# Decoder layer on one core: the 35 rounds of self-attention written out, and one transposition of the slot stage moved into the next projection

## The chip, the cores and the metric

The kernel runs on one core of one Trainium2 chip, as one program for a whole post-norm decoder layer. The metric is the device time of one execution in microseconds, from the kernel's runs on the chip; lower is better. The core's engines are TensorE (PE in the rows; PEld is its loading of weights), VectorE (DVE), ScalarE (ACT), GpSimd (POOL) and SyncE (SP, which here issues most DMAs). Each engine has its own stream of instructions, and they wait for each other by semaphores only.

## The reference, cut to what matters

```python
# x (8, 512, 512), ctx_1024 (8, 512, 512); H = 16 heads
# self-attention with relative positions, D = 32
scores = jnp.einsum('bhqd,bhkd->bhqk', q, k)
rel_q = jnp.einsum('bhld,lrd->bhlr', q, pos_emb)
rel_k = jnp.einsum('bhrd,lrd->bhlr', k, pos_emb)
probs = jax.nn.softmax((scores + rel_q + rel_k) / sqrt(D), axis=-1)
out = layernorm(ctx(probs, v) @ Wo + bo + x)
x = _layernorm(x + out)
...
x = _layernorm(x + cross_attention(x, ctx_1024))     # 16 heads of 64, causal
# slot layer: 16 slots per batch attend to the tokens, one expert per slot, tokens attend to the slots
o = q + _mha(q, x, x, d_Wq, ..., d_Wo, d_bo)          # q: slot_query, 16 rows per batch
...
x = _layernorm(x + _mha(x, o, o, c_Wq, ..., c_Wo, c_bo))
```

## The kernel before

The program is a row of stages with a barrier between them: `self_attention` (its first 1,900 us), `project_norm` (its output projection and two norms), `cross_attention`, `norm_and_slots` (cross-attention's projection and norm, together with the slots' attention over the tokens), `experts`, and `slots_to_tokens`. The change touches the first and the fourth.

**Self-attention.** The work is cut into 32 quads (`QUADS`): a quad is four heads of one batch. A round `g` of an engine is one call of its `quad(g, j)`, 16 steps `i` (four heads, four tiles of 128 query rows), and `j` is `g % 4`, which picks buffers. The stages of the pipeline lie up to two quads apart, so the rounds go from -2 to 32, 35 in all. In a step TensorE does `score` (L225, L227), `bands` for a later step (L251 to L257, the relative-position products that go out to DRAM and come back sheared by DMA), a share of the projections (L275, L286, L321, L324), and `turn` (L237), the transposition of an earlier tile of probabilities; VectorE's copy at L478 (`v_out`) stands once in each round, at its step 2. The order of these pieces is fixed by tables (`Q_AT`, `KV_AT`, `STACK_TICKS` and others), which the change leaves alone. `steps` is what calls `quad`, on each of the five engines: rounds -2, -1 and 0 are written out, rounds 1 to 24 are a hardware loop (`Fori`) of three passes whose body is eight rounds, and rounds 25 to 32 are written out again. Inside the loop `g` is a register, so the numbers that waits compare with and the addresses of some DMAs are worked out by register instructions; outside it they are constants.

**The slot stage.** `norm_and_slots` goes over 32 tiles of 128 tokens, one for each step `s`; four tiles are a batch `b`. On TensorE a step is `project(s)` (L1249, eight logical matmuls of 128x512 that the trace shows as 16), and `turn(s - 2)` (L1259, the transposition of a normed tile). Every fourth step adds `scores(b)` (L1292), the one after it `turn_probs(b, 0)` and `turn_probs(b, 1)` (both L1301: the batch's two tiles of slot probabilities are transposed, one after the other, into the same PSUM tile `ps_t`), and the next `mix(b)` (L1312). Between the two, ScalarE's `pt_out` (L1509) has to copy the first tile out of `ps_t`, and it does so behind the norm of a token tile (L1494) in its own queue.

Of the kernel before, what the change touches and what calls it, by code (L numbers as in the profile page):

```python
# [13 lines left out]
K4 = E // P  # L14
# [3 lines left out]
QUADS = B * (H // HQ)  # L18
# [31 lines left out]
def self_attention(nc, dr, sem, keep):  # L50
# [6 lines left out]
    with ExitStack() as ctx:  # L57
# [44 lines left out]

        def steps(e, quad):

            for g in (-2, -1, 0):
                quad(g, g % 4)
            with e.Fori(1, QUADS - 7, 8) as g:
                for j in range(8):
                    quad(g + j, (1 + j) % 4)
            for g in range(QUADS - 7, QUADS + 1):  # L110
                quad(g, g % 4)

        def ahead(g, j, i):
# [7 lines left out]
        def _(sp):  # L121
# [83 lines left out]
            for c in range(2):  # L205
                sp.dma_start(okv[c][:, :, :, :].rearrange("p a k n -> p (a k n)"), dr["b_wkv"](c))\
                    .then_inc(sem[f"a_okv_in{c}"], 16)
            steps(sp, quad)
            sp.wait_ge(sem["a_stored"], 16 * QUADS + 16)
            for i in range(2):  # L210
# [3 lines left out]
        def _(pe):  # L214
# [141 lines left out]

            pe.wait_ge(sem["a_wq_in"], 16 * K4)
            steps(pe, quad)

        @block.scalar  # L360
        def _(act):
# [64 lines left out]
            act.wait_ge(sem["a_cols_in"], 16)  # L426
            act.wait_ge(sem["a_bk_in"], 16)
            steps(act, quad)

        @block.vector  # L430
# [167 lines left out]
UNITS = B * T4  # L598
# [536 lines left out]
def norm_and_slots(nc, dr, sem, first, keep):  # L1135
# [5 lines left out]
    with ExitStack() as ctx:  # L1141
# [6 lines left out]
        R, CT, CH = 6, 4, 2 * K4  # L1148
        SCORES, TURNS, MIX = T4 + 3, T4 + 4, T4 + 5
# [33 lines left out]
        def at(s, lag):  # L1183

            return (s - lag) // T4 if (s - lag) % T4 == 0 and 0 <= s - lag < UNITS else None
# [55 lines left out]

        @block.tensor
        def _(pe):
            def project(u):
                pe.wait_ge(sem[f"f_in{u % R}"], 32 * (u // R) + 32)
                if u >= 2:
                    pe.wait_ge(sem["f_summed"], u - 1)
                for k in range(CH):
                    mm = pe.matmul(ps_o[u % 2][:, :], cT[u % CT][:, k, :], w[:, k, :], start=(k == 0), stop=(k == CH - 1))  # L1249
                mm.then_inc(sem["f_projected"], 1)  # L1250

            def turn(u):
                pe.wait_ge(sem["f_y"], u + 1)
                if u == 0:
                    pe.wait_ge(sem["f_const_in"], 16)
                if u:
                    pe.wait_ge(sem["f_yT"], u)
                for k in range(K4):
                    mm = pe.transpose(ps_y[:, k * P:(k + 1) * P], y[u // T4 % 2][:, u % T4, k * P:(k + 1) * P], ident[:, :])  # L1259
                mm.then_inc(sem["f_turned"], 1)  # L1260

            def queries():
                pe.wait_ge(sem["f_setup_in"], 64)
                for m in range(K4):
                    for k in range(K4):
                        mm = pe.matmul(ps_m[:, 0, m * NS:(m + 1) * NS], wq[:, k, m * P:(m + 1) * P], sqT[:, k, :],
                                       start=(k == 0), stop=(k == K4 - 1))
                mm.then_inc(sem["f_q_ready"], 1)

            def folded():  # L1270
                pe.wait_ge(sem["f_qd"], 1 + K4 * HQ)
                for m in range(K4):
                    mm = pe.matmul(ps_m[64 * (m % 2):64 * (m % 2) + 64, 1, m // 2:m // 2 + 1],
                                   qd[:, m, :, :].rearrange("p h s -> p (h s)"), cols[:, 1, m:m + 1],
                                   start=True, stop=True)
                mm.then_inc(sem["f_cb_ready"], 1)
                for k in range(K4):
                    for m in range(K4):
                        mm = pe.matmul(ps_s[:, k // 2, (k % 2) * HS + m * 64:(k % 2) * HS + (m + 1) * 64],
                                       wkT[:, m, k * P:(k + 1) * P], qd[:, m, :, :].rearrange("p h s -> p (h s)"),  # L1280
                                       start=True, stop=True)
                mm.then_inc(sem["f_a_ready"], 1)

            def scores(b):
                pe.wait_ge(sem["f_yT"], T4 * b + T4)
                if b == 0:
                    pe.wait_ge(sem["f_a"], 1)
                else:
                    pe.wait_ge(sem["f_scaled"], 2 * b)
                for i in range(2):  # L1290
                    for k in range(K4):
                        mm = pe.matmul(ps_s[:, i, :], a[:, k, i * P:(i + 1) * P], yT[b % 2][:, k, :],  # L1292
                                       start=(k == 0), stop=(k == K4 - 1))
                    mm.then_inc(sem["f_scored"], 1)

            def turn_probs(b, i):
                pe.wait_ge(sem["f_probs"], 2 * b + i + 1)
                if b or i:
                    pe.wait_ge(sem["f_pt"], 2 * b + i)
                for r in range(T4):  # L1300
                    mm = pe.transpose(ps_t[:, r * P:(r + 1) * P], sc[b % 2][:, i, r * P:(r + 1) * P], ident[:, :])  # L1301
                mm.then_inc(sem["f_probs_turned"], 1)

            def mix(b):
                pe.wait_ge(sem["f_pt"], 2 * b + 2)
                if b:
                    pe.wait_ge(sem["f_mixed_out"], b)
                else:
                    pe.wait_ge(sem["f_a"], 1)
                for k in range(K4):  # L1310
                    for r in range(T4):
                        mm = pe.matmul(ps_m[:, k // 2, (k % 2) * HS:(k % 2 + 1) * HS], y[b % 2][:, r, k * P:(k + 1) * P],  # L1312
                                       pt[:, r, :], start=(r == 0), stop=(r == T4 - 1))
                mm.then_inc(sem["f_mixed"], 1)

            pe.wait_ge(sem["f_w_in"], 16)
            for s in range(STEPS):
                if s < UNITS:
                    project(s)
                if s == SETUP:  # L1320
                    queries()
                if s == SETUP + 1:
                    folded()
                if at(s, TURNS) is not None:
                    turn_probs(at(s, TURNS), 0)
                if 0 <= s - 2 < UNITS:
                    turn(s - 2)
                if at(s, TURNS) is not None:
                    turn_probs(at(s, TURNS), 1)
                if at(s, SCORES) is not None:  # L1330
                    scores(at(s, SCORES))
                if at(s, MIX) is not None:
                    mix(at(s, MIX))
            pe.wait_ge(sem["f_mixed_out"], B)
            pe.wait_ge(sem["f_end_in"], 96)
            for m in range(K4):
                for k in range(K4):
                    for hh in range(HQ):
                        c = HQ * m + hh
                        mm = pe.matmul(ps_s[D * hh:D * (hh + 1), 0, m * SB:(m + 1) * SB], wv[:, k, c * D:(c + 1) * D],  # L1340
                                       mixed[:, :, k, c * NS:(c + 1) * NS].rearrange("p b s -> p s b"),
                                       start=(k == 0), stop=(k == K4 - 1))
            mm.then_inc(sem["f_cx_ready"], 1)
            pe.wait_ge(sem["f_cx"], 1)
            for m in range(K4):
                mm = pe.matmul(ps_s[:, 1, :], cx[:, m, :], wo[:, m, :], start=(m == 0), stop=(m == K4 - 1))
            mm.then_inc(sem["f_o_ready"], 1)
            pe.wait_ge(sem["f_h"], 3)
            for k in range(K4):
                mm = pe.transpose(ps_t[:, k * P:(k + 1) * P], h[:, k * P:(k + 1) * P], ident[:, :])  # L1350
# [851 lines left out]
```

## Time and profile before

| | |
|---|---|
| median of 3 runs | 3918.7 us (3915.43 to 3924.49) |
| profiled execution, its own time | 3919.53 us |
| its span, first to last instruction | 3917.9 us |
| mean granted clock of TensorE | 0.954 |
| instructions in the trace | 65,917 |
| busy: TensorE, VectorE, GpSimd, ScalarE | 3508.0, 2177.9, 1823.9, 1770.2 us |

The busy time of an engine is the sum over its instructions, and its share of the span says how near it is to being the bound on average. The granted clock is 1.00 where TensorE runs at its upper level of 2.4 GHz and 0.50 where it runs at 1.2 GHz. "Idle before" is the time that an engine stood still ahead of an instruction; the name behind the arrow is what ended it, and "issue" there means that nothing in the profile was being waited for.

### The profile page before, as it was taken

Reading aid. Unit: us, or ns where it says so; the run is one execution under the profiler, and the core shown is the slowest. Engines: PE = TensorE matmul, PEld = TensorE weight load, DVE = VectorE, ACT = ScalarE, POOL = GpSimd, SP = SyncE. Lnnn points to the kernel's source line nnn. Section 1 sums busy time; section 2 is a strip of 40 time slices with the busy share of each in tenths; the row PEclk is TensorE's granted clock in tenths of the full one; section 3 lists DMA queues with packets and bytes.
Section 4 is the critical chain, followed back from the end, with each engine's and each line's share of the span. In section 5 each row is a group of like instructions: output and inputs, shape, how many; then the busy total and the mean of one; then the engine's idle time right before and its main releaser. Section 6 shows DMA issues by size and latency. Waiting matters only on the chain. (4 is left out here: it accounts for less than half of the span.)

```text
span 3917.9 us, 65917 instructions
## 1 busy us (share of the span) xinstructions
PE 3508.0 (90%) x19744; PEld 2239.2 (57%) x19744; DVE 2177.9 (56%) x5890; ACT 1770.2 (45%) x3799; POOL 1823.9 (47%) x1652
## 2 busy tenths in 40 slices
PE   6999989999899999999897999999899986565588
PEld 4777767777677777777444555555455541111154
DVE  4666656666566666666686666666433321211267
ACT  4666656666566666666355555555212210000024
POOL 3666656666566666666325777777411100000012
PEclk8999999999999999999998999999999998888799
DMA  7999998999899999999793223222345319999914
GB/s 280 386 386 382 380 386 339 387 380 381 341 386 383 380 383 385 379 389 385 253 275 115 84 85 95 84 84 73 120 149 199 113 42 415 417 417 418 376 65 172
DMA packets 429722, 1091.96 MB, mean 279 GB/s; under 512 B 25152, under 2 KB 107584, under 8 KB 380224
## 3 DMA queue, kind: packets, MB, share of 16 engines
q1 hardware_dynamic: 412208, 1040.34, 71.0%
q10 hardware_dynamic: 16656, 47.19, 3.1%
q8 instruction: 162, 2.65, 0.3%
q14 instruction: 184, 1.51, 0.1%
q0 software_dynamic: 512, 0.26, 0.0%
HBM read 650.97 MB, written 436.73 MB: 278 GB/s over the span
## 5 line engine op out<-in xcount | busy, mean ns | idle before, releaser
L553 POOL TENSOR_SCALAR a_sc<-a_sc,a_inv 128x512 f32<-128x512 f32 x512 | 823.9, 1609 | 585.3 <-DVE a_inv L496 540.8
L505 DVE COPY a_pt<-a_ps_t 128x512 f32<-128x512 f32 x512 | 353.5, 690 | 547.8 <-PE a_ps_t L237 530.4
L1096 POOL TENSOR_SCALAR b_sc<-b_sc,b_inv 128x128 f32<-128x128 f32 (+3 forms) x512 | 547.3, 1086 | 181.1 <-DVE b_inv L1065 177.8
L375 ACT ACTIVATE a_stage_q<-a_ps_b 128x640 f32<-128x640 f32 x512 | 360.8, 705 | 587.6 <-PE a_ps_b L255 552.9
L1026 ACT ACTIVATE b_sc<-b_sc,b_mx 128x128 f32<-128x128 f32 (+3 forms) x512 | 282.0, 552 | 317.0 <-DVE b_mx L1059 316.7
L365 ACT ACTIVATE a_sc<-a_sc,a_mx 128x512 f32<-128x512 f32 x512 | 370.0, 723 | 54.8 <-DVE a_mx L489 51.4
L489 DVE CUSTOM_DVE_ANT_0 a_sc<-a_ps_s,a_rq 128x512 f32<-128x512 f32 x512 | 353.1, 690 | 74.6 <-PE a_ps_s L227 59.3
L375 ACT ACTIVATE a_stage_k<-a_ps_b 128x640 f32<-128x640 f32 x512 | 357.4, 698 | 0.0
L237 PEld LDWEIGHTS a_ps_t<-a_ident,a_sc 128*128 128x128 f32 x2048 | 247.6, 141 | 146.5 <-issue 141.1
L1059 DVE CUSTOM_DVE_ANT_0 b_sc<-b_ps_s,b_mask 128x128 f32<-128x128 f32 (+3 forms) x512 | 229.5, 488 | 166.0 <-PE b_ps_s L974 162.2
L237 PE MATMUL a_ps_t<-a_ident,a_sc 128*128 128x128 f32 x2048 | 308.9, 274 | 8.8 <-DVE a_pt L505 8.8
L227 PE MATMUL a_ps_s<-a_ident,a_rk 128*128 128x128 f32 x2048 | 307.6, 273 | 0.0
L324 PEld LDWEIGHTS a_ps_o<-a_okv,keep 128*128 128x128 f32 x2048 | 263.2, 191 | 76.8 <-issue 72.2
L227 PEld LDWEIGHTS a_ps_s<-a_ident,a_rk 128*128 128x128 f32 x2048 | 256.3, 141 | 37.8 <-issue 1.2
L1710 POOL DMA_DIRECT2D y<-d_y x16 | 8.6, 535 | 577.1 <-DVE d_y L1681 577.1
L275 PE MATMUL a_ps_c<-a_xT,keep 128*128 128x512 f32 x512 | 256.4, 605 | 21.9 <-DVE a_lo_q L459 12.1
L324 PE MATMUL a_ps_o<-a_okv,keep 128*128 128x128 f32 x2048 | 269.5, 276 | 1.8 <-ACT a_kv L397 1.8
L321 PE MATMUL a_ps_o<-keep,a_okv 128*128 128x512 f32 x512 | 266.6, 607 | 0.4 <-ACT a_kv L400 0.4
L960 PE MATMUL b_ps_q<-b_xT,keep 128*128 128x512 f32 x512 | 260.5, 612 | 6.8 <-PEq L2124 6.8
L225 PE MATMUL a_ps_s<-a_ks,a_qs 128*128 128x512 f32 x512 | 248.1, 485 | 17.1 <-issue 11.7
L1072 DVE COPY b_pt<-b_ps_t 128x128 f32<-128x128 f32 (+3 forms) x512 | 226.9, 485 | 63.7 <-PE b_ps_t L982 63.7
L1249 PE MATMUL f_ps_o<-keep,f_cT 128*128 128x512 f32 x512 | 234.8, 614 | 9.3 <-DMA f_x<-x 9.3
(215 smaller groups left out, 6227.0 us busy)
## 6 DMA issues: line engine op xcount, KB each, us to landing
band_q<-a_stage_q SPq DMA_DIRECT2D x128, 1280.0 KB, 6.8
band_k<-a_stage_k SPq DMA_DIRECT2D x128, 1280.0 KB, 9.9
a_rk<-band_k SPq DMA_DIRECT2D x128, 1024.0 KB, 12.7
a_rq<-band_q SPq DMA_DIRECT2D x256, 512.0 KB, 13.4
d_w<-in_e_W SPq DMA_DIRECT2D x24, 4096.0 KB, 42.9
d_wg<-in_e_Wg SPq DMA_DIRECT2D x16, 4096.0 KB, 28.5
keep<-in_e_W SPq DMA_DIRECT2D x8, 4096.0 KB, 36.3
a_okv<-in_b_wkv ACTq DMA_DIRECT2D x62, 512.0 KB, 7.9
```

The lines of the kernel that those rows point to most:

```text
L227: mm = pe.matmul(out[:, r * P:(r + 1) * P], rk[h][:, r, t * P:(t + 1) * P], ident[:, :], is_transpose=True, start=False, stop=(r == T4 - 1))
L237: mm = pe.transpose(ps_t[:, r * P:(r + 1) * P], sc[i % SC][:, r * P:(r + 1) * P], ident[:, :])
L321: mm = pe.matmul(ps_o[:, :], okv[c][:, 0, n, :], oc[:, n, :], start=(n == 0), stop=(n == K4 - 1))
L324: mm = pe.matmul(ps_o[:, n * P:(n + 1) * P], oc[:, k, n * P:(n + 1) * P], okv[c][:, 1, k, :], start=(k == 0), stop=(k == K4 - 1))
L365: act.activation(sc[n][:, :], sc[n][:, :], ACT.Exp, bias=mx[:, n:n + 1], scale=-1.0, accum_out=sm[:, n:n + 1]).then_inc(sem["a_exped"], 1)
L375: act.activation(st[h % 2][:, t, :], src, ACT.Copy).then_inc(sem[f"a_{kind}_staged"], 1)
L489: dve.tensor_tensor_reduce(out=sc[n][:, :], in0=ps_s[i % 2][:, :], in1=rq[rn][:, i % 2, :], scale=-SCALE_A, scalar=BIG, op0=ALU.add, op1=A ...
L505: dve.tensor_copy(pt[:, h % 2, :, t * P:(t + 1) * P], ps_t[:, :].rearrange("p (r n) -> p r n", r=T4)).then_inc(sem["a_pt_out"], 1)
L553: pool.tensor_scalar(sc[n][:, :], sc[n][:, :], inv[:, n:n + 1], None, ALU.mult)\
L960: mm = pe.matmul(ps_q[:, :], wq[:, j % XP, k, :], xT[j // XP][:, k, :], start=(k == 0), stop=(k == K4 - 1))
L1026: act.activation(sc[j % 2][i][:, 0:width(i)], sc[j % 2][i][:, 0:width(i)], ACT.Exp, bias=mx[j % 2][:, i:i + 1], scale=-1.0, accum_out=sm[j ...
L1096: pool.tensor_scalar(sc[j % 2][i][:, 0:width(i)], sc[j % 2][i][:, 0:width(i)], inv[j % 2][:, i:i + 1], None, ALU.mult).then_inc(sem["b_nor ...
```

## The change

Two edits. `steps` calls `quad` for all 35 rounds with numbers instead of a loop, on all five engines, so there is no jump and no register in self-attention. And in the slot stage `project` is cut into two halves of four matmuls, and `turn_probs(b, 1)` goes from the end of its step to between the halves of the next step's projection.

```diff
         def steps(e, quad):
 
-            for g in (-2, -1, 0):
-                quad(g, g % 4)
-            with e.Fori(1, QUADS - 7, 8) as g:
-                for j in range(8):
-                    quad(g + j, (1 + j) % 4)
-            for g in range(QUADS - 7, QUADS + 1):
+            for g in range(-2, QUADS + 1):
                 quad(g, g % 4)
...
-            def project(u):
-                pe.wait_ge(sem[f"f_in{u % R}"], 32 * (u // R) + 32)
-                if u >= 2:
-                    pe.wait_ge(sem["f_summed"], u - 1)
-                for k in range(CH):
+            def project(u, half):
+                if half == 0:
+                    pe.wait_ge(sem[f"f_in{u % R}"], 32 * (u // R) + 32)
+                    if u >= 2:
+                        pe.wait_ge(sem["f_summed"], u - 1)
+                for k in range(K4 * half, K4 * half + K4):
                     mm = pe.matmul(ps_o[u % 2][:, :], cT[u % CT][:, k, :], w[:, k, :], start=(k == 0), stop=(k == CH - 1))
-                mm.then_inc(sem["f_projected"], 1)
+                if half:
+                    mm.then_inc(sem["f_projected"], 1)
...
                 if s < UNITS:
-                    project(s)
+                    project(s, 0)
+                if at(s, MIX) is not None:
+                    turn_probs(at(s, MIX), 1)
+                if s < UNITS:
+                    project(s, 1)
...
                     turn_probs(at(s, TURNS), 0)
                 if 0 <= s - 2 < UNITS:
                     turn(s - 2)
-                if at(s, TURNS) is not None:
-                    turn_probs(at(s, TURNS), 1)
                 if at(s, SCORES) is not None:
                     scores(at(s, SCORES))
```

TensorE at the end of the loop's body in the kernel before: the last products of a round, then the loop's own two instructions, and then the written-out round 25.

```order
L324 MATMUL a_ps_o<-a_okv,keep 128x128 x4
L237 MATMUL a_ps_t<-a_ident,a_sc 128x128 x4
L107 REGISTER_ALU
L107 COMPARE_AND_BRANCH
L225 MATMUL a_ps_s<-a_ks,a_qs 128x512
L227 MATMUL a_ps_s<-a_ident,a_rk 128x128 x4
L251 MATMUL a_ps_b<-a_eq,a_qs 128x384
```

TensorE in the changed kernel where round 8 ends and round 9 begins, the place where the loop jumped back (lines of the changed kernel stand five lower in self-attention).

```order
L319 MATMUL a_ps_o<-a_okv,keep 128x128 x4
L232 MATMUL a_ps_t<-a_ident,a_sc 128x128 x4
L220 MATMUL a_ps_s<-a_ks,a_qs 128x512
L222 MATMUL a_ps_s<-a_ident,a_rk 128x128 x4
L246 MATMUL a_ps_b<-a_eq,a_qs 128x384
L249 MATMUL a_ps_b<-a_eq,a_qs 128x256
```

The matmuls and their order are the same in both; the register instruction and the branch between two rounds are gone, and so are those within the rounds.

TensorE in the slot stage before, from one batch's probabilities (L1301) to its mixing (L1312); f_ps_t is `ps_t`, f_ps_o the projection's tile, f_ps_y that of a normed token tile.

```order
L1249 MATMUL f_ps_o<-keep,f_cT 128x512 x8
L1301 MATMUL f_ps_t<-d_ident,f_sc 128x128 x4
L1259 MATMUL f_ps_y<-d_ident,f_y 128x128 x4
L1301 MATMUL f_ps_t<-d_ident,f_sc 128x128 x4
L1249 MATMUL f_ps_o<-keep,f_cT 128x512 x8
L1259 MATMUL f_ps_y<-d_ident,f_y 128x128 x4
L1312 MATMUL f_ps_m<-f_pt,f_y 128x256 x16
```

The same stretch in the changed kernel.

```order
L1245 MATMUL f_ps_o<-keep,f_cT 128x512 x8
L1298 MATMUL f_ps_t<-d_ident,f_sc 128x128 x4
L1256 MATMUL f_ps_y<-d_ident,f_y 128x128 x4
L1245 MATMUL f_ps_o<-keep,f_cT 128x512 x4
L1298 MATMUL f_ps_t<-d_ident,f_sc 128x128 x4
L1245 MATMUL f_ps_o<-keep,f_cT 128x512 x4
L1256 MATMUL f_ps_y<-d_ident,f_y 128x128 x4
L1309 MATMUL f_ps_m<-f_pt,f_y 128x256 x16
```

The second tile's transposition has moved behind four matmuls of the projection that used to follow it. For the last two batches there is no projection left in the next step, and the order is what it was.

## Rows read from the trace of the kernel before

**Rows 1.** The page: busy time, two DMA queues, the slot stage's projection.
```profile
PE 3508.0 (90%) x19744; PEld 2239.2 (57%) x19744; DVE 2177.9 (56%) x5890; ACT 1770.2 (45%) x3799; POOL 1823.9 (47%) x1652
...
q8 instruction: 162, 2.65, 0.3%
q14 instruction: 184, 1.51, 0.1%
...
L1249 PE MATMUL f_ps_o<-keep,f_cT 128*128 128x512 f32 x512 | 234.8, 614 | 9.3 <-DMA f_x<-x 9.3
```

**Rows 2.** Windows: engines' busy time, then granted clock, DMA share, GB/s.
```profile
580.00:590.00 10.00, 5.74 (x19) 4.56 (x20) 2.72 (x6) 2.60 (x5) 2.77 (x3) 0.50 0.67 239
1521.15:1747.28 226.13, 223.71 (x1473) 172.91 (x1472) 147.49 (x349) 142.82 (x281) 142.81 (x129) 1.00 1.01 386
```

**Rows 3.** Timeline of TensorE behind the loop's first jump: start, duration, idle before.
```profile
581.20 0.79 PE L225 MATMUL a_ps_s<-a_ks,a_qs 128*128 128x512 f32 x1 [5.83 <-issue]
...
586.22 0.37 PE L254 MATMUL a_ps_b<-a_eq,a_qs 128*128 128x256 f32 x1 [3.06 <-issue]
```

**Rows 4.** Timeline of VectorE: the copy that stands once in each round.
```profile
527.92 0.69 DVE L478 COPY a_v<-a_ps_c 128x512 f32<-128x512 f32 x1 [0.45 <-PE a_ps_c L286]
598.06 0.69 DVE L478 COPY a_v<-a_ps_c 128x512 f32<-128x512 f32 x1 [0.45 <-PE a_ps_c L286]
...
767.74 0.69 DVE L478 COPY a_v<-a_ps_c 128x512 f32<-128x512 f32 x1 [0.46 <-PE a_ps_c L286]
825.17 0.69 DVE L478 COPY a_v<-a_ps_c 128x512 f32<-128x512 f32 x1 [0.45 <-PE a_ps_c L286]
...
995.22 0.69 DVE L478 COPY a_v<-a_ps_c 128x512 f32<-128x512 f32 x1 [0.45 <-PE a_ps_c L286]
1065.67 0.69 DVE L478 COPY a_v<-a_ps_c 128x512 f32<-128x512 f32 x1 [0.46 <-PE a_ps_c L286]
...
1521.15 0.69 DVE L478 COPY a_v<-a_ps_c 128x512 f32<-128x512 f32 x1 [0.52 <-PE a_ps_c L286]
...
1747.28 0.69 DVE L478 COPY a_v<-a_ps_c 128x512 f32<-128x512 f32 x1 [0.52 <-PE a_ps_c L286]
```

**Rows 5.** Timeline of the slot stage: one batch from norm to mixing.
```profile
2963.15 0.60 PE L1259 MATMUL f_ps_y<-d_ident,f_y 128*128 128x128 f32 x4
...
2970.45 0.60 PE L1259 MATMUL f_ps_y<-d_ident,f_y 128*128 128x128 f32 x4
...
2984.63 0.60 PE L1301 MATMUL f_ps_t<-d_ident,f_sc 128*128 128x128 f32 x4
...
2985.06 0.60 PE L1259 MATMUL f_ps_y<-d_ident,f_y 128*128 128x128 f32 x4
...
2987.57 0.58 ACT L1509 ACTIVATE f_pt<-f_ps_t 128x512 f32<-128x512 f32 x1
2988.29 1.08 PE L1301 MATMUL f_ps_t<-d_ident,f_sc 128*128 128x128 f32 x4 [2.63 <-ACT f_pt L1509]
...
2989.17 8.01 PE L1249 MATMUL f_ps_o<-keep,f_cT 128*128 128x512 f32 x16
...
2997.02 0.60 PE L1259 MATMUL f_ps_y<-d_ident,f_y 128*128 128x128 f32 x4
...
3011.24 0.60 PE L1259 MATMUL f_ps_y<-d_ident,f_y 128*128 128x128 f32 x4
```

**Rows 6.** The same timeline: L1259 beside the probabilities of batches 0, 3 and 5.
```profile
2890.01 0.60 PE L1259 MATMUL f_ps_y<-d_ident,f_y 128*128 128x128 f32 x4
...
3033.15 0.60 PE L1259 MATMUL f_ps_y<-d_ident,f_y 128*128 128x128 f32 x4
...
3043.71 0.60 PE L1259 MATMUL f_ps_y<-d_ident,f_y 128*128 128x128 f32 x4
...
3128.21 0.60 PE L1259 MATMUL f_ps_y<-d_ident,f_y 128*128 128x128 f32 x4
...
3140.28 0.60 PE L1259 MATMUL f_ps_y<-d_ident,f_y 128*128 128x128 f32 x4
```

## Prediction

> **What bounds the kernel now.** I read the page first. TensorE is busy for 90% of the span, and no other engine for more than 56% [rows 1], so time is to be had where TensorE stands still or runs slowly. Windows of 10 us over self-attention came next. They are full of TensorE work at a clock of 1.00 nearly everywhere, and fall to about half at two places, near 575 and near 1045 us; the first is shown, with 5.74 us of work at a clock of 0.50 [rows 2]. The timeline at that place shows TensorE idle for 5.83 us and, five microseconds later, for another 3.06 us, both times put down to "issue": nothing in the profile was being waited for [rows 3]. VectorE and ScalarE stand still at the same moment. It is the point where all five engines jump back to the head of the loop: three passes make two jumps, and there are two such places. The loop is entered and left without a gap of this kind.
>
> In the slot stage I read the projection's group and the timeline of one batch. The projection waited for a DMA only once, 9.3 us at the stage's start [rows 1], and TensorE goes without a gap through the steps, but for one place in each batch: 2.63 us ahead of the second transposition of probabilities, until ScalarE has copied the first tile out [rows 5].
>
> **The change, part by part. The jumps.** The copy at L478 is a clock for the rounds. The round with the first jump takes 598.06 - 527.92 = 70.14 us, and the round at the same place of the pattern of four, without a jump, 825.17 - 767.74 = 57.43; the jump costs 12.71 us. The second: 1065.67 - 995.22 = 70.45, less 57.43, is 13.02 us [rows 4]. That is all of it: the two idles (8.9 us in the first case) and TensorE's work at half clock between and behind them. The sum is 25.7 us. After the edit no engine has a branch there, and the instructions of both sides are the ones that run today. I take all of it, since no other work lies under it: TensorE is what stands still, and the rounds before and after are full.
>
> **The register instructions.** Written-out rounds exist in the trace of before: 25 to 32. Four of them take 1747.28 - 1521.15 = 226.13 us; the same four places in the loop take 825.17 - 598.06 = 227.11. That is 0.98 us for four rounds, and 24 rounds move over, so 6 x 0.98 = 5.9 us. Another way to read it: from 598.06 to 1065.67 are eight rounds, 467.61 us with one jump, without it 454.59, against twice 226.13 = 452.26; 2.3 us for eight rounds or 7.0 for 24 [rows 4]. From below nothing, if the difference is the place in the stage and not the registers. I take 5.9, which both readings are near, with 0 and 7.0 as bounds.
>
> What could take it back is the fetching of instructions. The two instruction queues moved 2.65 + 1.51 = 4.16 MB for 65,917 instructions, 63 bytes each [rows 1]: what runs is fetched as it runs, in the loop on each pass too. So the written-out program fetches about as much, and somewhat less for the register instructions that go. The written-out rounds 25 to 32 ran at full clock with 223.71 us of TensorE work in 226.13 [rows 2], so fetching straight code was hidden under them. The DMA side can't catch its breath any more at a jump, and its engines read 1.01 busy in those rounds [rows 2]. But rounds 17 to 32 already run 16 in a row, and their length doesn't creep up; 32 in a row should not either.
>
> The Trainium skill (Runtime: NRT & Kernel Launch, Instruction fetch mechanics) says that prefetch is sequential and that a taken branch out of the present pages waits for the fetch of its target page. By that rule one jump is one wait; the row shows two, 5.83 and 3.06 us [rows 3]. If the second were an ordinary page boundary and stayed, some 3 us and a part of the slow clock would be kept at each place, and the gain would be 25.7 less 3.1 and 3.1, or 19.5, and the sum 48.6. The same instructions ran in the first pass, entered without a jump, and had no such idle, so I side with the trace and count both.
>
> **The moved transposition.** From one L1259 to the next over a plain step takes 2970.45 - 2963.15 = 7.30 us, and a transposition of four adds 2985.06 - 2984.63 = 0.43. So the stretch from L1259 of the probabilities' step to the next should take 7.73 us with `turn_probs` in it. It takes 2997.02 - 2985.06 = 11.96 us [rows 5], and 3043.71 - 3033.15 = 10.56 in the mildest batch, 3140.28 - 3128.21 = 12.07 in the last that counts [rows 6]. The difference between 10.56 and the others is the clock: behind the idle of 2.63 us the projection took 2997.02 - 2989.17 = 7.85 us until the next L1259, against 7.30 - 0.43 = 6.87 in a plain step, and the transposition itself 1.08 instead of 0.60 [rows 5]. For all six batches: 3128.21 - 2890.01 = 238.20 us over five periods is 47.64 each [rows 6]; without the stall a period is 7.73 + (3011.24 - 2997.02 = 14.22) + 7.30 + (2985.06 - 2970.45 = 14.61) = 43.86 [rows 5]. Five times 3.78 is 18.9, and the sixth batch gives 12.07 - 7.73 = 4.3. Together 23.2 us. Batches 6 and 7 keep their order and give nothing.
>
> Does the moved piece wait anew? Its first half-projection starts at 2985.06 + 0.43 and takes (7.30 - 0.43) / 2 = 3.44 us, so TensorE comes to it at 2988.93. ScalarE's copy ends at 2987.57 + 0.58 = 2988.15, and the row shows the transposition starting at 2988.29 [rows 5]. The margin is 0.64 us. The copy stands behind the norm of a token tile (L1494) on ScalarE, and nothing of the edit moves either. The second copy now waits until about 2989.4 and ends by 2990.1; behind it in ScalarE's queue stands the square root for the tile whose projection ends only near 2992.8, so nothing waits for ScalarE. `mix` needs the copy after a further transposition of tokens, at about 2993. The cover of the new copy is thus a half-projection of 3.44 us against 0.6 us of copying. If the margin fell away, what is late next is TensorE itself, by tenths of a microsecond.
>
> From below: if only the stall and not the clock came back, it is six times 10.56 - 7.73 = 2.83, 17.0 us [rows 5, 6]. From above nothing beyond 23.2, because no other gap is left there.
>
> The weights of the first expert are loaded in the middle of this stage, well ahead of its end, and the later stages keep their lengths and only start earlier.
>
> **The sum.** The profiled execution took 3919.5 us (span 3917.9 and 1.6 around it), the median of the runs is 3918.7, 0.8 lower. 25.7 + 5.9 + 23.2 = 54.8 us, so 3864.7 by the profiled execution and 3863.9 by the median. I say 3864. The bounds of this case: 19.5 + 0 + 17.0 = 36.5 us of gain at worst, 25.7 + 7.0 + 23.2 = 56 at best, 3863 to 3882 by the median, and 3 us on either side for the spread of the runs: 3860 to 3885.
>
> **Rivals.** (1) The straight rounds become bound by DMA. DMA engines read busy throughout [rows 2], and the pauses of some 12 us at the jumps are the only rest. If they were what keeps the band reads in time, the 25.7 us would be given back as waits at the scores: 3864 + 26 = 3890. Against it: 16 rounds in a row without drift. 7 in 100. (2) The slot stage keeps its wait: the moved transposition meets a late copy, or the clock falls for another reason. With the 17.0 us it is 3870, inside my range; with nothing gained there 3887. The margin of 0.64 us speaks against, but it is thin, and the early batches might differ. 7 in 100 for the loss of most of it. (3) The other side: fetching the written-out code isn't hidden. A stall of the kind seen at a jump, 12.9 us, then stands at places in the straight code. With 55 us to win, counting the two that go, it takes more than four such stalls in 24 rounds to make the kernel slower; one in every third round is eight, 103 us, and 3967. Rounds 25 to 32 had none in eight rounds, and neither had the first pass of the loop. 3 in 100. (4) The edit doesn't do what it says. The instructions in order show no branch left in self-attention, and the moved rows; 1 in 100, with 3919. My forecast has the remaining 82 in 100.
>
> **How the numbers follow.** What a measurement of this kernel can tell from no change is about 0.2%, 7.8 us: 3911 to 3926.5. The main case and the first two rivals are all below 3911. So faster 0.95, the same 0.02, slower 0.03. The range takes the main case's 3860 to 3885 and widens it below to 3856, for a gain in straight rounds that I undersized, and above to 3890, where the first two rivals end.
>
> **What would show it right or wrong.** In the profile after: no "issue" idle of several microseconds on TensorE in self-attention, and no fall of the clock near 575 or 1045 us; the copy at L478 (then L473) every 55.9 to 57.4 us in all rounds; in the slot stage no wait of the transpositions for ScalarE's copy in batches 0 to 5, and 43.9 us for a batch. Wrong would be: waits of the scores for the sheared bands, "issue" idles at regular distances in the straight rounds, or a new idle of TensorE between the halves of a projection.

## The result, and the profile after

The changed kernel takes 3861.97 us in the median of four runs (3859.88 to 3866.55), the kernel before 3921.59 in the same comparison (3915.43 to 3928.5). The ratio is 0.9856, with a 95% interval of 0.9843 to 0.9868: 1.4% faster, by 52 to 62 us. The profiled executions have spans of 3861.9 and 3917.9 us, 56.0 apart, against a forecast of 54.8.

The page of the changed kernel, where it answers to [rows 1]:

```profile
PE 3488.0 (90%) x19744; PEld 2230.2 (58%) x19744; DVE 2173.7 (56%) x5890; ACT 1768.0 (46%) x3799; POOL 1823.7 (47%) x1652
...
q8 instruction: 155, 2.54, 0.3%
q14 instruction: 150, 1.23, 0.1%
...
L1245 PE MATMUL f_ps_o<-keep,f_cT 128*128 128x512 f32 x512 | 230.9, 603 | 8.5 <-DMA f_x<-x 8.5
```

The counts of the working instructions are the same; what fell is TensorE's busy time, by 20 us, at the places where it ran at half clock before (below). The two instruction queues moved less, not more: 2.54 + 1.23 = 3.77 MB where it was 4.16.

Windows of the changed kernel, the first where the jump was, the second over four rounds that used to be in the loop:

```profile
580.00:590.00 10.00, 9.44 (x64) 6.17 (x63) 5.87 (x13) 4.80 (x9) 7.14 (x7) 1.00 1.03 390
1036.61:1263.09 226.48, 223.65 (x1473) 172.87 (x1472) 147.16 (x349) 142.93 (x281) 142.49 (x129) 1.00 1.01 385
```

Where the clock was 0.50 and TensorE did 5.74 us of work in ten [rows 2], it reads 1.00 and 9.44. The timeline of VectorE, with the copy that stands once in each round (rounds 1, 8, 9 and 25; its line is five lower than before):

```profile
130.08 0.69 DVE L473 COPY a_v<-a_ps_c 128x512 f32<-128x512 f32 x1 [0.52 <-PE a_ps_c L281]
...
525.92 0.69 DVE L473 COPY a_v<-a_ps_c 128x512 f32<-128x512 f32 x1 [0.52 <-PE a_ps_c L281]
583.19 0.69 DVE L473 COPY a_v<-a_ps_c 128x512 f32<-128x512 f32 x1 [0.52 <-PE a_ps_c L281]
...
1489.68 0.69 DVE L473 COPY a_v<-a_ps_c 128x512 f32<-128x512 f32 x1 [0.52 <-PE a_ps_c L281]
```

The round that jumped is now 57.27 us long instead of 70.14 [rows 4], and TensorE has no idle put down to "issue" in self-attention. From the first of these rows to the last are 24 rounds, 1359.60 us.

What the jump waited for can be read in the kernel before. The queue q8 carries TensorE's instructions, and q14 those of other engines: with TensorE alone written out q8 falls from 2.65 to 2.54 MB and q14 stays at 1.51, and with the other four written out it is q14 that falls, to 1.23, and q8 that stays (both kernels stand below). The DMA view of the kernel before, first for the 5.83 us of the first idle (575.37 to 581.20), then for the 3.06 of the second (583.17 to 586.22):

```profile
q8 instruction: 1, 0.02, 1.0%
```

```profile
q8 instruction: 1, 0.02, 2.7%
```

Each idle holds one packet of q8, of 16 KB (at 578.57 and 583.59 us in the trace), and ends 1.7 and 1.3 us behind that packet's end. It is the same at all eleven jumps of TensorE in the four kernels that have them (this one and three of the experiments): 22 idles, 22 packets, and 1.3 to 1.8 us from a packet's end to TensorE's next matmul. In the rounds of the changed kernel the packets of q8 come every 13 to 25 us, and TensorE does not stop for them. So both idles read as waits for instructions; no run changed the fetching alone.

The slot stage. First one batch in the timeline, to be read beside [rows 5], then windows of the changed kernel and of the kernel before, each from the first batch's first transposition of probabilities to the last L1259 (L1256) that has a projection ahead of it:

```profile
2991.11 0.60 PE L1298 MATMUL f_ps_t<-d_ident,f_sc 128*128 128x128 f32 x4
...
2991.55 0.60 PE L1256 MATMUL f_ps_y<-d_ident,f_y 128*128 128x128 f32 x4
...
2991.99 3.60 PE L1245 MATMUL f_ps_o<-keep,f_cT 128*128 128x512 f32 x8
...
2994.06 0.58 ACT L1508 ACTIVATE f_pt<-f_ps_t 128x512 f32<-128x512 f32 x1
2995.42 0.60 PE L1298 MATMUL f_ps_t<-d_ident,f_sc 128*128 128x128 f32 x4
2995.86 3.60 PE L1245 MATMUL f_ps_o<-keep,f_cT 128*128 128x512 f32 x8
2996.06 0.60 ACT L1508 ACTIVATE f_pt<-f_ps_t 128x512 f32<-128x512 f32 x1 [1.43 <-PE f_ps_t L1298]
...
2999.29 0.60 PE L1256 MATMUL f_ps_y<-d_ident,f_y 128*128 128x128 f32 x4
```

```profile
2859.50:3108.56 249.06, 249.06 (x782) 135.54 (x781) 82.56 (x184) 52.03 (x88) 25.31 (x20) 1.00 0.42 149
```

```profile
2889.57:3161.80 272.23, 256.47 (x782) 139.02 (x781) 82.58 (x184) 52.03 (x88) 25.31 (x20) 0.97 0.38 136
```

The copy ends at 2994.64 and TensorE comes for the second transposition at 2995.42, without a wait. The distance from L1256 to L1256 is 7.74 us, where it was 11.96. Over the whole stretch TensorE is busy 249.06 of 249.06 us at clock 1.00; before it was 256.47 of 272.23 at 0.97. The stretch is 23.17 us shorter with the same 782 matmul records.

Where the rest lies is read from four anchors: the first matmul of the output projection behind self-attention, and one near the end of the slot stage, in the kernel before and after:

```profile
1908.44 5.70 PE L713 MATMUL na_ps_o<-keep,na_cT 128*128 128x512 f32 x8 [9.24 <-DMA na_xT<-in_xT]
...
3226.20 0.72 PE L1350 MATMUL f_ps_t<-d_ident,f_x 128*128 128x128 f32 x4 [4.29 <-DVE f_x L1477]
```

```profile
1878.48 5.64 PE L708 MATMUL na_ps_o<-keep,na_cT 128*128 128x512 f32 x8 [9.21 <-DMA na_xT<-in_xT]
...
3171.86 0.66 PE L1349 MATMUL f_ps_t<-d_ident,f_x 128*128 128x128 f32 x4 [4.29 <-DVE f_x L1476]
```

Self-attention ends 29.96 us earlier. At the second anchor it is 54.34, so 24.4 lie between, nearly all in the slot stage; the last 1.7 us up to 56.0 came in the experts' and tokens' stages, which the change leaves alone.

### The profile page after: what moved, and what is told of

Its sections match the earlier page's. It is cut to its first block and busy times, and to the rows that moved or that the text cites. A ratio compares the mean times of both kernels' runs of the same rounds, so it can differ in the third digit from the quotient of the medians.

```text
span 3861.9 us, 63144 instructions
## 1 busy us (share of the span) xinstructions
PE 3488.0 (90%) x19744; PEld 2230.2 (58%) x19744; DVE 2173.7 (56%) x5890; ACT 1768.0 (46%) x3799; POOL 1823.7 (47%) x1652
## 3 DMA queue, kind: packets, MB, share of 16 engines
q8 instruction: 155, 2.54, 0.3%
q14 instruction: 150, 1.23, 0.1%
## 5 line engine op out<-in xcount | busy, mean ns | idle before, releaser
L270 PE MATMUL a_ps_c<-a_xT,keep 128*128 128x512 f32 x512 | 256.5, 605 | 22.6 <-DVE a_lo_q L454 12.5
## 6 DMA issues: line engine op xcount, KB each, us to landing
a_rk<-band_k SPq DMA_DIRECT2D x128, 1024.0 KB, 12.9
d_wg<-in_e_Wg SPq DMA_DIRECT2D x16, 4096.0 KB, 28.4
```

## The experiments

The theory is the forecast's: two jumps at about 12.9 us, register instructions, and six stalls with a slow clock behind them. Its rivals are that the gain comes from one of the edits alone or from the registers, that the price belongs to the loop and not to the jump, and that something other than the copy's place held the transposition. Except where it is said otherwise, a kernel has the other edit as in the kernel before.

**Each edit alone.** The first has the written-out `steps`, the second the halved projection with `turn_probs` in its middle; each is one half of the diff that is shown above.

> Only self-attention's rounds are written out; the slot stage is that of before. Theory (two jumps at 12.9 us each, register instructions some 4 to 6 us, parts add up): 30 us faster than before, ratio 0.9923. Rival (the two edits help each other, or the gain lies mostly in the slot stage): less than 20 us.

Measured: 3886.97 us (3879.98 to 3893.96) against 3917.46 beside it, 30.5 us less; ratio 0.9916 (0.9898 to 0.9934). The theory's 30 holds, and its 24 rounds take 1359.52 us (131.56 to 1491.08), as in the changed kernel.

> Only the second tile of probabilities is moved into the next projection; self-attention loops as before. Theory (six stalls of 2.63 us and the slow clock behind four of them): 23 to 24 us faster than before, ratio 0.9940, with no clock below 1.00 in the slot stage between its start and batch 6. Rival (the clock falls in that stage for another reason): 17 us or less, ratio above 0.9955.

Measured: 3895.63 us (3892.71 to 3898.25), 21.8 us less; ratio 0.9942 (0.9925 to 0.9958). The theory's 23 to 24 lie within its interval, and the rival's ratio above 0.9955 is only just inside; the stage decides: its first six batches are 43.87 us apart as in the changed kernel, and the mean granted clock from the stage's start to the seventh is 1.00. The two edits alone make 52.3 us, and both together 59.6 in one comparison and 57.2 in another (below). With intervals of some 6 us on each, the parts add up within the noise.

**Registers without a jump.** One pass over a body of 24 rounds: every wait and address still has its register.

```diff
-            with e.Fori(1, QUADS - 7, 8) as g:
-                for j in range(8):
+            with e.Fori(1, 3, 2) as g:
+                for j in range(24):
                     quad(g + j, (1 + j) % 4)
```

> Self-attention's 24 rounds as one pass of a loop whose body has all 24: g is still a register in every wait and address, but no jump is taken. Slot stage of before. Theory (jumps cost 25.7 us, registers 4 to 6): 26 us faster than before, 4 to 6 us slower than the written-out kernel of the same call. Rival (the register instructions are what cost, and the idle at the jump is made up elsewhere): no more than 10 us faster than before.

Measured: 3895.25 us (3893.9 to 3898.04), 22.2 us less than before; ratio 0.9945 (0.9929 to 0.9962), and 8.3 us behind the written-out kernel, more than was expected. The stage itself is less noisy to read than the whole. The copies of rounds 1 and 25 in this kernel, and then that of round 1 in the kernel before:

```profile
130.23 0.69 DVE L478 COPY a_v<-a_ps_c 128x512 f32<-128x512 f32 x1 [0.45 <-PE a_ps_c L286]
...
1493.12 0.69 DVE L478 COPY a_v<-a_ps_c 128x512 f32<-128x512 f32 x1 [0.52 <-PE a_ps_c L286]
```

```profile
129.85 0.69 DVE L478 COPY a_v<-a_ps_c 128x512 f32<-128x512 f32 x1 [0.45 <-PE a_ps_c L286]
```

That is 1362.89 us for the 24 rounds. Written out they are 1359.60, so the registers cost 3.3 us. In the kernel before the same rounds, from 129.85 to 1521.15 us, took 1391.30, so taking two jumps cost 28.4. The other 5 us between the two medians are not seen in the profiles: the profiled executions took 3893.9 and 3893.96 us, and there it was the written-out kernel whose `project_norm` was longer, 186.1 against 181.1 us with the same code. That stage alone varies by as much as is to be explained.

Where the 3.3 us lie can be read on TensorE. Once in each round it waits for VectorE's copy of the probabilities; in the kernel before, and in the changed one:

```profile
189.50 1.92 PE L307 MATMUL a_ps_c<-a_pt,a_v 128*32 128x512 f32 x16 [0.71 <-DVE a_pt L505]
```

```profile
189.50 1.92 PE L302 MATMUL a_ps_c<-a_pt,a_v 128*32 128x512 f32 x16 [0.56 <-DVE a_pt L500]
```

The wait is 0.70 to 0.83 us in every round with registers, this kernel's too, and 0.56 to 0.60 in written-out rounds; with TensorE alone or the other four alone written out (below) it is 0.62 to 0.68. Some 0.15 us in each of 24 rounds is 3.6, so the registers' price lies at this one place of a round.

**More jumps.** The body is four rounds, so five jumps are taken.

```diff
-            with e.Fori(1, QUADS - 7, 8) as g:
-                for j in range(8):
+            with e.Fori(1, QUADS - 7, 4) as g:
+                for j in range(4):
```

> The loop's body is four rounds instead of eight, so five jumps are taken instead of two; slot stage of before. Theory (a fixed price of 12.9 us for each jump taken): 38.6 us slower than before, ratio 1.0098. Rival A (a shorter body is still at hand for the engines and its jump is cheap): faster than before by up to 25 us. Rival B (the price belongs to the loop as such, not to the jump): no change.

Measured: 3952.14 us (3950.18 to 3957.27), 34.7 us more; ratio 1.0091 (1.0073 to 1.0108). Both rivals fall. Around the second jump, timeline of TensorE and of VectorE's copies:

```profile
594.11 0.79 PE L225 MATMUL a_ps_s<-a_ks,a_qs 128*128 128x512 f32 x1 [6.35 <-issue]
598.57 0.37 PE L254 MATMUL a_ps_b<-a_eq,a_qs 128*128 128x256 f32 x1 [2.49 <-issue]
```

```profile
540.35 0.69 DVE L478 COPY a_v<-a_ps_c 128x512 f32<-128x512 f32 x1 [0.46 <-PE a_ps_c L286]
609.87 0.69 DVE L478 COPY a_v<-a_ps_c 128x512 f32<-128x512 f32 x1 [0.45 <-PE a_ps_c L286]
```

The theory's 38.6 is 4 us too much; of the 34.7, 31.6 lie in the 24 rounds (1422.93 us). All five jumps look like this, with two idles put down to "issue", 5.8 to 6.4 us and 2.5 to 3.1. This round takes 69.52 us; the five are 69.89, 69.52, 69.45, 69.25 and 69.30, against 57.40 for the round of that place without a jump, so a jump costs 12.1 us on average.

**Whose jump it is.** `steps` gets a flag, and the engines named are written out while the others loop.

```diff
-        def steps(e, quad):
+        def steps(e, quad, written=False):
 
+            if written:
+                for g in range(-2, QUADS + 1):
+                    quad(g, g % 4)
+                return
...
-            steps(pe, quad)
+            steps(pe, quad, True)
```

> TensorE's rounds are written out, the other four engines still loop; slot stage of before. Theory (every engine stands still at its own jump for some 6 us, TensorE for a second time for 3 us, and TensorE has no slack): TensorE now waits for VectorE and ScalarE at their jumps, so about half of the two jumps' price comes back: 8 to 14 us faster than before. Rival A (TensorE's own fetch is all that counts): 26 us or more. Rival B (any engine's jump costs the full price): 0 to 3 us.

Measured: 3904.65 us (3900.56 to 3908.08) against 3920.32, 15.7 us less; ratio 0.9957 (0.9944 to 0.9971). A little above the 8 to 14 of the theory: the 24 rounds take 1374.65 us, 16.65 less than before, of which the two jumps give 12.2, rounds 6, 14 and 22, which are no longer than others here, 2.6 (below), and the shorter wait for the copy of probabilities (0.63 us) the rest. The timeline at the first jump:

```profile
581.25 0.60 ACT L404 ACTIVATE a_kv<-a_ps_o 128x512 f32<-128x512 f32 x1 [5.26 <-issue]
...
581.99 2.05 PE L325 MATMUL a_ps_o<-keep,a_okv 128*128 128x512 f32 x2 [4.38 <-ACT a_kv L404]
...
582.38 0.69 DVE L509 COPY a_pt<-a_ps_t 128x512 f32<-128x512 f32 x1 [5.79 <-issue]
```

TensorE goes on for 2.4 us, and then stands still for ScalarE, which stands still at its own jump. The copies of VectorE put this round at 64.08 us against 57.33: 6.75 us, half the price.

> TensorE still loops, the other four engines are written out; slot stage of before. Theory (TensorE's own two idles, 5.83 and 3.06 us, and the half clock between them are the price, and the others stand still under them): close to before, 0 to 5 us faster, from the register instructions of the others. Rival (the others' jumps add to TensorE's): 12 us or more faster.

Measured: 3918.06 us (3914.35 to 3920.61) against 3920.32; ratio 0.9996 (0.9986 to 1.0006). No change in the whole, as the theory had it; the 24 rounds are 3.5 us shorter (1387.82). The timeline at the first jump of this kernel:

```profile
576.54 0.69 DVE L509 COPY a_pt<-a_ps_t 128x512 f32<-128x512 f32 x1
...
581.45 0.79 PE L229 MATMUL a_ps_s<-a_ks,a_qs 128*128 128x512 f32 x1 [6.06 <-issue]
...
583.31 0.69 DVE L493 CUSTOM_DVE_ANT_0 a_sc<-a_ps_s,a_rq 128x512 f32<-128x512 f32 x1 [6.07 <-PE a_ps_s L231]
...
587.28 0.37 PE L258 MATMUL a_ps_b<-a_eq,a_qs 128*128 128x256 f32 x1 [3.88 <-issue]
```

VectorE does the copy at 576.54 at once, where the kernel before held it until 582.32 (its row has 5.82 of issue), and it gains nothing by that: it then waits 6.07 us for TensorE. Its stalls and TensorE's lay over one another. Only with all five written out did the whole price go; which engines besides TensorE are needed for that was not tried one by one.

**The margin of the moved transposition.** The changed kernel, cut after two matmuls.

```diff
-                for k in range(K4 * half, K4 * half + K4):
+                for k in ((0, 1) if half == 0 else range(2, CH)):
```

> The changed kernel with the projection cut after two of its eight matmuls instead of four. Theory (the margin ahead of the first copy is 0.64 us, and half of a half-projection is 1.72 us): TensorE comes 1.1 us too early and waits 1.1 us in each of six batches, 6 to 7 us slower than the changed kernel, or up to 14 if the clock falls behind a wait of this length. Rival (the copy is ready whenever TensorE is away from it for a moment): no change.

Measured: 3868.79 us (3867.36 to 3869.51); ratio to the kernel before 0.9866 (0.9847 to 0.9886). That is 6.8 us above the median of the changed kernel in the main comparison, as the theory had it. The second transposition of batch 1 in the timeline:

```profile
2904.22 0.63 PE L1298 MATMUL f_ps_t<-d_ident,f_sc 128*128 128x128 f32 x4 [0.91 <-ACT f_pt L1508]
```

TensorE waits 0.91 us in this batch and the ones after it, and 1.27 in batch 0; the clock stays up behind a wait of this length. The batches are 44.97 us apart where they were 43.87, so a batch loses 1.10 us against 1.1 expected; the idle in the row reads a little less than the delay, since the ends of matmuls in the profile are modelled. The margin was real, and it is thin: a cut at four has it, one at two has not.

**The wait removed from the other side.** Self-attention written out; TensorE's order of before; ScalarE copies the first tile before the square root and the norm.

```diff
             for s in range(STEPS):
+                if at(s, TURNS) is not None:
+                    pt_out(at(s, TURNS), (0,))
                 if s < UNITS:
                     std(s)
...
                 if at(s, TURNS) is not None:
-                    pt_out(at(s, TURNS))
+                    pt_out(at(s, TURNS), (1,))
```

> Self-attention written out; in the slot stage TensorE's order is that of before, and ScalarE copies the first tile of probabilities out before the square root and the norm of its step, not behind them. Theory (the 2.63 us were the copy's place in ScalarE's queue): TensorE waits some 0.5 us instead of 2.63 in batches 0 to 5 and the clock stays up, 18 to 20 us faster than the written-out kernel with the old slot stage, 4 us slower than the changed kernel. Rival (delaying the norm delays the token tiles' transpositions and so TensorE elsewhere): no faster than the written-out kernel.

Measured: 3863.4 us (3860.29 to 3866.21); ratio 0.9853 (0.9833 to 0.9874). Its timeline:

```profile
2944.64 0.60 PE L1296 MATMUL f_ps_t<-d_ident,f_sc 128*128 128x128 f32 x4
...
2945.08 0.60 PE L1254 MATMUL f_ps_y<-d_ident,f_y 128*128 128x128 f32 x4
...
2945.28 0.60 ACT L1504 ACTIVATE f_pt<-f_ps_t 128x512 f32<-128x512 f32 x1 [4.98 <-PE f_ps_t L1296]
...
2946.02 0.63 PE L1296 MATMUL f_ps_t<-d_ident,f_sc 128*128 128x128 f32 x4 [0.34 <-ACT f_pt L1504]
...
2953.36 0.60 PE L1254 MATMUL f_ps_y<-d_ident,f_y 128*128 128x128 f32 x4
```

The copy starts 0.64 us after the transposition instead of 2.94 [rows 5], TensorE waits 0.34 us instead of 2.63, and the clock doesn't fall. This shows the cause: the wait came from the copy's place in ScalarE's queue. From L1254 to L1254 are 8.28 us, against 7.74 in the changed kernel: 0.54 us for each of six batches, 3.2 us. In the whole time this doesn't show, since the two kernels differ by 1.4 us. The norm that it delays costs nothing: the batches are 44.40 us apart, 0.53 more than in the changed kernel. The rival falls, and the expected 4 us can't be told from none.

**The loops of the other stages.** In `project_norm`, `cross_attention` and `experts` the loops become plain `for` loops over numbers, in the changed kernel (the first of three alike):

```diff
-            for s in range(R):
-                step(s, s)
-            with e.Fori(R, UNITS - R, R) as s:
-                for j in range(R):
-                    step(s + j, j)
-            for s in range(UNITS - R, UNITS + R):
+            for s in range(UNITS + R):
                 step(s, s % R)
```

> The changed kernel with the loops of project_norm (one jump taken), cross_attention and experts (six jumps) written out too; only GpSimd's own loop in cross_attention stays. Theory (a jump costs some 9 to 13 us where TensorE has no slack): one jump in project_norm goes, 5 to 10 us, and the experts stage, which waits for its weights, gives nothing: 5 to 12 us faster than the changed kernel, that is 62 to 70 us faster than before. Rival (these stages wait for DMA at those places anyway, so the jumps are hidden): within 3 us of the changed kernel.

Measured: 3866.79 us (3852.73 to 3872.19) against 3915.85; ratio 0.9878 (0.9857 to 0.9899). Its profiled execution was its fastest, 3852.73, and showed `project_norm` 5.4 us shorter than the changed kernel's; but the median is 49.1 us below the kernel before, where 62 to 70 were expected, and shows no gain over the changed kernel. So the experts' loop was put back, the other two stayed written out, and that kernel was set beside the changed one.

> The changed kernel once more, to stand beside the next one. 56 to 60 us faster than before.

> The changed kernel with the loops of project_norm and cross_attention written out (GpSimd's own loop there stays), and the experts' loop left as it is. Theory (the one jump of project_norm cost 5 us and the one idle in cross_attention 2 to 4, as the profile of the kernel without loops reads): 6 to 10 us faster than the changed kernel of the same call. Rival (those stages differ by as much from one execution to the next): within 3 us.

Measured, against 3916.21 for the kernel before: the changed kernel 3859.03 us (3856.99 to 3865.09), ratio 0.9856 (0.9839 to 0.9873), 57.2 us less as expected; with those loops written out 3860.96 (3856.6 to 3872.37), ratio 0.9866 (0.9847 to 0.9885). The expected 6 to 10 us did not come. The two are the same, and the rival holds: what one profile showed of `project_norm` was the spread of that stage. From the first projection to the first matmul of cross-attention it took 180.7 us in this last kernel (1878.3 to 2059.0), and 177.3 in the changed one beside it (1878.5 to 2055.8), with a jump. No version tried is faster than the changed kernel.

## Why the prediction was right

**The jumps.** Forecast 25.7 us for two. The rounds that jumped did fall by 12.87 us, from 70.14 to 57.27, and the 24 rounds in one pass against the loop give 28.4 us. The term was somewhat small, because more than those two rounds was longer: in the kernel before, rounds 6, 14 and 22, the sixth of each pass, were 1.1, 0.3 and 1.2 us longer than the ones at the same place elsewhere, 2.6 in all, and in one pass they are no more than 0.3 longer. At their start ScalarE's issue of the next batch's input held it for 5.30, 4.49 and 5.37 us, where it is 2.7 to 3.1 in the written-out kernels. Why is open. In the one pass with registers five of the seven such holds are 2.7 to 2.9 us, and the two in rounds 6 and 22 are 4.4 and 4.3; with TensorE alone written out all three are 4.0 to 4.1, and no round is longer.

**The second idle.** From the rule in the Trainium skill (Runtime: NRT & Kernel Launch, Instruction fetch mechanics) that a taken branch waits for the fetch of its target page, the forecast drew a reading by which one jump is one wait, and 3.1 us would have stayed at each place. It sided with the trace instead and counted both idles. That was right: neither is left after, and five jumps showed both, five times. The trace agrees with the rule in the first idle, which holds a packet of q8; the second idle holds a packet of its own, which the forecast did not look for.

**The registers.** Forecast 5.9 us with 0 and 7.0 as bounds; measured 3.3. Both readings were too large because both compared with the same four written-out rounds, 226.13 us, which began with one of 55.92, where other rounds at that place take 56.4 to 56.5 in the loop and 56.3 to 56.4 outside it (TensorE does not wait for the copy of probabilities in it); the second reading also took in the 0.3 us of round 14. With the jumps the term comes to 31.7 us over the 24 rounds, against 31.6 forecast: two sizes off by some 2.7 us in opposite directions, and that they cancel is luck.

**Given back.** Of the 31.7 us self-attention kept 29.96. The first rounds began 0.2 us later; rounds 25 to 30 took 282.86 us instead of 282.49; and from the last copy to the output projection it took 1.1 us longer, 105.94 us instead of 104.80. The last can't be put down to the change: in the profiles of all kernels here, looping or not, that stretch takes 104.8 to 106.0 us. TensorE does wait there for the sheared bands, three times, but it did so before as well; the first of the three in the kernel before, and in the changed one:

```profile
1845.48 0.50 PE L225 MATMUL a_ps_s<-a_ks,a_qs 128*128 128x512 f32 x1 [1.33 <-DMA a_rk<-band_k]
```

```profile
1814.40 0.50 PE L220 MATMUL a_ps_s<-a_ks,a_qs 128*128 128x512 f32 x1 [1.35 <-DMA a_rk<-band_k]
```

The three are 1.33, 1.18 and 1.39 us before, and 1.35, 1.22 and 1.36 after. In the 24 rounds of the former loop there is none. So the first rival, that DMA binds without the pauses, does not show at all, though the DMA engines read 1.01 busy.

**The slot stage.** Forecast 23.2 us from six batches, measured 23.17, with the stall and the half clock both gone; a batch takes 43.87 us, where 43.86 was forecast. The margin was forecast as 0.64 us from the time at which a transposition can follow the copy, 0.14 behind the copy's end. Reckoned in the same way it is 2995.42 - 2994.64 - 0.14 = 0.64. The cut at two showed from the other side that it decides: the forecast's arithmetic gives 1.08 us a batch there, and it was 1.10.

**Fetching** did not hold up the straight code: no "issue" idle stands on TensorE in its 35 rounds, as the written-out rounds of before had promised.

The sum was 54.8 us against 56.0 between the profiles and 59.6 between the medians. The 3.6 us between these two lie in the spread of the runs; in the last comparison the difference of the medians was 57.2.

## What to carry to other kernels

Here a hardware loop's jump back showed as an "issue" idle on TensorE, VectorE and ScalarE at once, a second one on TensorE, and a low clock behind it. Price it by the length of the rounds with and without it, and multiply by the jumps that are taken, not by the loops. "issue" alone is not enough to know it by: in the experts' stage of the changed kernel TensorE has idles so called, one of 3.89 us before L1634, at a matmul that waits for a semaphore and with no packet of an instruction queue in it. Writing the loop out paid where TensorE had no slack, and gave nothing measurable in `project_norm` and `cross_attention`. It takes more than one engine: TensorE alone gave half, and the other four alone gave nothing. And a short wait for a buffer can be taken away from either side, by putting other work between the two users or by moving the copy up in its engine's queue; compute the margin before choosing the place.

## What was not expected of the hardware

The clock's fall behind the same idle was not the same each time. With 2.62 to 2.63 us of it the stretch from L1259 to L1259 was 10.56 us in two of six batches and 11.96 to 12.25 in four, and behind waits of 0.91 to 1.27 us the clock never fell. The five jumps of the shorter loop, each with idles of about 8.9 us in all, show a granted clock of 0.51 to 0.57 in the ten us behind the first idle, against 0.50 at both jumps of the kernel before, so most of it at 1.2 GHz, and cost 11.9 to 12.5 us; for one of them:

```profile
594.11:604.11 10.00, 7.50 (x30) 5.92 (x31) 3.38 (x7) 2.59 (x5) 2.88 (x3) 0.57 0.51 176
```

And a body half as long made a jump hardly cheaper: 12.1 us on average with four rounds, 12.7 and 13.0 with eight.
